# The expert loop's turn from half 0 to half 1: half 0's last groups in turns with half 1's first three, and two separate root chains

## The chip, the core and the metric

The kernel runs on one core of a Trainium2 chip. The metric is the device time of one execution in microseconds (us), the median of several runs. The engines' names in the rows are PE (TensorE), PEld (TensorE's weight loads), DVE (VectorE), ACT (ScalarE), POOL (GpSimd) and SP (SyncE, which only issues DMAs here). ACTq marks DMAs that ScalarE issues.

## The reference

The program is a small "macaron" stack on x of 2 x 1024 tokens with 128 channels: a squared-ReLU feed-forward, softmax attention, the feed-forward again, an expert layer, linear attention, and the same expert layer again.

```python
x = x + 0.5 * ffn0(_layernorm(x))
x = x + attn0(_layernorm(x))
x = x + 0.5 * ffn0(_layernorm(x))
x = x + 0.5 * experts(_layernorm(x))
x = x + linear_attention(_layernorm(x))
x = x + 0.5 * experts(_layernorm(x))
```

The change touches only `experts`:

```python
logits = x_flat @ Wr + br                       # 16 experts
topk_w, topk_idx = top_k(softmax(logits), 2)    # weights made to sum to 1
h = gelu(_layernorm(x_flat @ W1[e] + b1[e], g1[e], be1[e]))
y = sum over the 2 chosen e of topk_w * (h @ W2[e] + b2[e])
```

## The kernel before, in words

The tokens are worked on in two halves of 1024 (the batch's two sequences). Both expert stages run the same code. For each half VectorE works out a slot for each token and choice, so that the tokens of one expert lie together, padded to tiles of 128 rows. GpSimd then sends the rows there with 16 indirect DMAs (`moe_pool_send`, L1157), SyncE loads them back as tiles (L1185), the loop below works on them, ScalarE's queue stores the results (L1192), and GpSimd fetches each token's two rows with 16 indirect DMAs (`moe_pool_fetch`, L1173). It fetches for half 0 once all of half 0's stores have landed, then for half 1 once all of half 1's have. VectorE adds them to x (L1456, L1461).

There are 31 tiles for each half, in 8 groups of 4 (`NGR`; the last has 3). The loop runs over 16 groups: 0 to 7 are half 0's, 8 to 15 half 1's. A group u passes these steps, by the names of the code:

- TensorE: `turn_in(u)` (L1211), 4 transposes of the loaded rows; waits for the load.
- ScalarE: `rows(u)` (L1347), copies them from PSUM.
- TensorE: `hidden(u)` (L1228), the product with the tile's own W1; waits for `rows(u)` and, as it writes the PSUM bank that group u - 4 used, for that group to be scaled.
- VectorE: `summed(u)` (L1406), statistics of each tile; then one root chain of 16 small instructions (L1419 to L1422, then `rsqrt` L233 to L239) for a pair of groups; then `scaled(u)` (L1430).
- TensorE: `turn(u)` (L1238), 4 transposes; ScalarE: `gelu(u)` (L1357), one ACTIVATE for each tile.
- TensorE: `out(u)` (L1252), the product with W2; waits for `gelu(u)` and, since there is one bank for it, for `out_in(u - 1)`.
- ScalarE: `out_in(u)` (L1366), copy to SBUF; then `store(u)` (L1192).

Each engine does its instructions in the order written, so a wait in one holds up all behind it. `LEAD` is 3: TensorE does `hidden(u + 3)` ahead of `turn(u)`. Only group 8 is treated apart before: its `turn_in` and `rows` stand behind `out(3)` and `out_in(3)`, since half 1's rows come late. VectorE takes the groups as 0, then (1, 2), (3, 4), (5, 6), (7, 8), ... (13, 14), then 15, with one root chain for each.

Of the kernel before, what the change touches and what calls it, by code (L numbers as in the profile page):

```python
# [57 lines left out]
def build(nc, A):  # L58
    with ExitStack() as ctx:
# [3 lines left out]
        def sem(name):  # L63
            return ctx.enter_context(nc.semaphore(name))
# [292 lines left out]
        class Ffn:  # L357
# [3 lines left out]
            k, r, v = sem("f_k"), sem("f_r"), sem("f_v")  # L361
# [602 lines left out]
        NGR = (NTL + 3) // 4  # L964
        LEAD = 3
# [234 lines left out]
        def moe_tensor(pe, pair, between):  # L1200
            u0 = NGR * pair[0].i
            last = u0 + 2 * NGR
            where = {}

            def turn_in(u):
                m, g = pair[(u - u0) // NGR], (u - u0) % NGR
                pe.wait_ge(t.xg[g], 16 * (m.i + 1))
                if u >= u0 + 2:
                    pe.wait_ge(t.xtc, u - 1)
                for j in range(tiles_in(g)):  # L1210
                    ins = pe.transpose(ps[:, TURN_IN_BANKS[u % 2], j * P:(j + 1) * P], t_xg[:, m.b, g, j, :], cc("ident"))  # L1211
                ins.then_inc(t.xt, 1)

            def hidden(u):
                m, g = pair[(u - u0) // NGR], (u - u0) % NGR
                k = tiles_in(g)
                if g == 0:
                    pe.wait_ge(m.tab, m.i + 1)
                regs = [pe.alloc_register(f"e{u}_{j}") for j in range(4)]
                pe.load(regs, r_tab[m.b][0:1, 4 * g:4 * g + 4])  # L1220
                at = [pe.snap(r, min_val=0, max_val=(NE - 1) * P) for r in regs]
                where[u] = regs, at
                pe.wait_ge(t.xtc, u + 1)
                if u >= u0 + 4:
                    pe.wait_ge(t.z, u - 3)
                bank = HIDDEN_BANKS[u % 4]
                for j in range(k):
                    ins = pe.matmul(ps[:, bank, j * P:(j + 1) * P], t_xt[:, u % 2, j * P:(j + 1) * P],  # L1228
                                    w1[:, :, :].rearrange("c e f -> c (e f)")[:, bass.ds(at[j], P)], start=True, stop=True)
                ins.then_inc(t.h, 1)  # L1230

            def turn(u):
                g = (u - u0) % NGR
                if u > u0 and u != last - 2:
                    pe.wait_ge(t.ac, u if u < last - 1 else u - 1)
                pe.wait_ge(t.z, u + 1)
                for j in range(tiles_in(g)):
                    ins = pe.transpose(ps[:, turn_bank(last - u), j * P:(j + 1) * P], t_z[:, u % 4, j, :], cc("ident"))  # L1238
                ins.then_inc(t.zt, 1)

            def out(u):
                m, g = pair[(u - u0) // NGR], (u - u0) % NGR
                k = tiles_in(g)
                pe.wait_ge(t.ac, u + 1)
                bank = out_bank(last - u)
                if u == last - 1:
                    pe.wait_ge(t.yc, u - 1)
                elif u >= u0 + 1 and u != last - 2:
                    pe.wait_ge(t.yc, u)
                regs, at = where.pop(u)  # L1250
                for j in range(k):
                    ins = pe.matmul(ps[:, bank, j * P:(j + 1) * P], t_a[:, u % 2, j * P:(j + 1) * P],  # L1252
                                    w2[:, :, :].rearrange("c e f -> c (e f)")[:, bass.ds(at[j], P)], start=True, stop=True)
                ins.then_inc(t.y, 1)
                for r in regs:
                    pe.free_register(r)

            def counts_read(m):
                pe.wait_ge(m.pick, m.i + 1)
                pe.wait_ge(m.gsel, m.i + 1)  # L1260

            pe.wait_ge(pair[0].slot, pair[0].i + 1)
            counts_read(pair[0])
            pe.wait_ge(s_w1, 1)
            turn_in(u0)
            keep_clock(pe, HIDDEN_BANKS[3], 2)
            hidden(u0)
            turn_in(u0 + 1)
            between(0)
            turn_in(u0 + 2)  # L1270
            hidden(u0 + 1)
            turn_in(u0 + 3)
            hidden(u0 + 2)
            between(1)
            keep_clock(pe, HIDDEN_BANKS[3], 6)
            pe.wait_ge(pair[1].slot, pair[1].i + 1)
            for u in range(u0, last - LEAD):
                hidden(u + LEAD)
                if u + LEAD + 1 < last and u + LEAD + 1 != u0 + NGR:
                    turn_in(u + LEAD + 1)  # L1280
                turn(u)
                if u == u0:
                    counts_read(pair[1])
                else:
                    out(u - 1)
                if u + LEAD + 1 == u0 + NGR:
                    turn_in(u + LEAD + 1)
            out(last - LEAD - 1)
            turn(last - 3)
            turn(last - 2)  # L1290
            out(last - 3)
            turn(last - 1)
            out(last - 2)
            out(last - 1)
# [43 lines left out]
        def moe_scalar(act, pair, between):  # L1338
            u0 = NGR * pair[0].i
            last = u0 + 2 * NGR  # L1340

            def rows(u):
                k = tiles_in(u)
                act.wait_ge(t.xt, u + 1)
                if u >= u0 + 2:
                    act.wait_ge(t.h, u - 1)
                nc.scalar.activation(t_xt[:, u % 2, 0:P * k], ps[:, TURN_IN_BANKS[u % 2], 0:P * k], ACT.Identity,  # L1347
                                     bias=cc("ident")[:, 0:1]).then_inc(t.xtc, 1)

            def gelu(u):  # L1350
                m, g = pair[(u - u0) // NGR], (u - u0) % NGR
                act.wait_ge(t.zt, u + 1)
                if u >= u0 + 2:
                    act.wait_ge(t.y, u - 1)
                for j in range(tiles_in(g)):
                    k = 4 * g + j
                    ins = nc.scalar.activation(t_a[:, u % 2, j * P:(j + 1) * P], ps[:, turn_bank(last - u), j * P:(j + 1) * P], ACT.Gelu,  # L1357
                                               bias=r_sel[m.b][:, 1, k:k + 1], scale=r_sel[m.b][:, 0, k:k + 1])
                ins.then_inc(t.ac, 1)

            def out_in(u):
                k = tiles_in(u)
                act.wait_ge(t.y, u + 1)
                if u >= 4:
                    act.wait_ge(t.ys[u % 4], 16 * (u // 4))
                nc.scalar.activation(t_y[:, u % 4, 0:k, :], ps[:, out_bank(last - u), 0:P * k].rearrange("p (j f) -> p j f", f=P), ACT.Copy)\  # L1366
                    .then_inc(t.yc, 1)

            for u in range(u0, u0 + LEAD + 1):
                rows(u)  # L1370
            between()

            def store(u):
                moe_scalar_store(act, pair[(u - u0) // NGR], (u - u0) % NGR)

            for u in range(u0, last - LEAD):
                if u >= u0 + 2:
                    store(u - 2)
                if u + LEAD + 1 < last and u + LEAD + 1 != u0 + NGR:
                    rows(u + LEAD + 1)  # L1380
                gelu(u)
                if u > u0:
                    out_in(u - 1)
                if u + LEAD + 1 == u0 + NGR:
                    rows(u + LEAD + 1)
            out_in(last - 4)
            store(last - 5)
            gelu(last - 3)
            store(last - 4)
            gelu(last - 2)  # L1390
            out_in(last - 3)
            gelu(last - 1)
            store(last - 3)
            out_in(last - 2)
            store(last - 2)
            out_in(last - 1)
            store(last - 1)

        def moe_vector_tiles(dve, vs, pair, slots, behind):
            u0 = NGR * pair[0].i  # L1400
# [31 lines left out]
                    bc(t_rs[:, at, pos:pos + k].unsqueeze(2), [P, k, P]), ALU.mult).then_inc(t.z, 1)  # L1432

            last = u0 + 2 * NGR - 1
            for u in range(u0 - 1, last + 1, 2):
                groups = range(max(u, u0), min(u + 1, last) + 1)
                for v in groups:
                    summed(v)
                dve.wait_ge(t.ss, groups[-1] + 1)
                if u < u0:  # L1440
                    vs.finish_both(slots, Chain(rstds(groups[0], groups[-1])))
                else:
                    vs.finish(Chain(rstds(groups[0], groups[-1])))
                for v in groups:
                    scaled(v)
# [1076 lines left out]
```

## Time and profile before

| what | value |
|---|---|
| median of 3 runs | 601.48 us (598.48 to 602.64) |
| the profiled execution's own time | 601.2 us |
| its span in the trace | 599.0 us |
| busy: PE, DVE, ACT, POOL | 81%, 78%, 52%, 27% of the span |
| first expert loop in the trace | about 322 to 386 us |
| second expert loop | about 509 to 570 us |
| fetches for half 1 to the end | 573.4 to 599.0 us |

The busy shares are means over the whole program, in which attention takes the larger part (to about 290 us). For the change the two expert loops and what follows each of them have to be read by themselves, instruction by instruction.

### The profile page before, as it was taken

Reading aid. Unit: us, or ns where it says so; the run is one execution under the profiler, and the core shown is the slowest. Engines: PE = TensorE matmul, PEld = TensorE weight load, DVE = VectorE, ACT = ScalarE, POOL = GpSimd, SP = SyncE. Lnnn points to the kernel's source line nnn. Section 1 sums busy time; section 2 is a strip of 40 time slices with the busy share of each in tenths; the row PEclk is TensorE's granted clock in tenths of the full one; section 3 lists DMA queues with packets and bytes.
Section 4 is the critical chain, followed back from the end, with each engine's and each line's share of the span. In section 5 each row is a group of like instructions: output and inputs, shape, how many; then the busy total and the mean of one; then the engine's idle time right before and its main releaser. Section 6 shows DMA issues by size and latency. Waiting matters only on the chain.

```text
span 599.0 us, 9248 instructions
## 1 busy us (share of the span) xinstructions
PE 487.4 (81%) x2996; PEld 259.4 (43%) x2996; DVE 468.1 (78%) x1248; ACT 312.5 (52%) x613; POOL 158.8 (27%) x198
## 2 busy tenths in 40 slices
PE   6787989999999999899788789748786887789720
PEld 3452422222222232244364679535435444679610
DVE  4978898988878988465887978697977776888852
ACT  2355456777776777688232658527143202468800
POOL 5020030010000110001274702773101055630775
PEclk8888999999999999999987979987989888999975
DMA  6006500049705003000235295511000012454542
GB/s 209 3 1 162 96 2 0 19 103 194 259 2 146 2 0 72 2 0 2 67 131 163 82 277 162 154 48 27 2 1 0 2 36 68 145 166 139 155 127 66
DMA packets 55356, 49.31 MB, mean 82 GB/s; under 512 B 4958, under 2 KB 47502, under 8 KB 54926
## 3 DMA queue, kind: packets, MB, share of 16 engines
q1 hardware_dynamic: 34686, 31.15, 18.8%
q0 software_dynamic: 4240, 9.45, 5.7%
q10 hardware_dynamic: 16384, 8.13, 4.5%
q8 instruction: 25, 0.41, 0.3%
q14 instruction: 21, 0.17, 0.1%
HBM read 25.85 MB, written 20.59 MB: 78 GB/s over the span
## 4 chain that ended last, share of the span: by engine, by line
PE 37%; DVE 28%; POOL 11%; issue 9%; ACT 9%; DMA 4%; ACTq 1%; SPq 0%; POOLq 0%; DVEq 0%
PE ps L814 9%; DVE arena L862 8%; PE ps L804 7%; PE ps L761 7%; POOL rows_in L1157 7%; ACT arena L1357 5%; POOL arena L1173 2%; DVE stat L257 2%; ACT arena L1366 1%; POOL small L249 1%; DMA row<-in_rows 1%; PE ps L575 1%; DVE arena L1905 1%; DMA arena<-rows_in 1%; DVE xl L285 1%
## 5 line engine op out<-in xcount | busy, mean ns | idle before, releaser
L862 DVE TENSOR_REDUCE arena<-ps 128x1 f32<-128x1024 f32 x128 | 150.8, 1219 | 25.0 <-PE ps L761 24.7
L927 ACT ACTIVATE arena<-ps 128x512 f32<-128x512 f32 x256 | 138.4, 602 | 55.1 <-PE ps L804 52.8
L804 PE MATMUL ps<-arena 99*128 99x512 bf16 x256 | 85.5, 383 | 1.1 <-ACT arena L927 1.0
L761 PE MATMUL ps<-arena 96*128 96x512 bf16 x256 | 76.5, 381 | 7.0 <-DVE arena L862 6.7
L1173 POOL DMA_INDIRECT arena<-rows_out,route x64 | 61.2, 956 | 66.4 <-DMA rows_out<-arena 47.1
L1157 POOL DMA_INDIRECT rows_in<-xl,route x64 | 62.4, 976 | 55.2 <-DVE route L1113 37.1
L814 PE MATMUL ps<-arena 128*32 128x512 f32 x512 | 68.2, 605 | 1.9 <-ACT arena L923 1.3
L804 PEld LDWEIGHTS ps<-arena 99*128 99x128 bf16 x256 | 22.2, 98 | 72.9 <-ACT arena L927 48.9
L249 POOL TENSOR_TENSOR small<-small,nhalf 128x8 f32<-128x8 f32 x11 | 18.2, 1657 | 123.4 <-DVE small L271 123.3
L1357 ACT ACTIVATE arena<-ps,route 128x128 f32<-128x128 f32 x124 | 46.4, 461 | 5.7 <-PE ps L1238 5.7
L202 PE MATMUL ps<-zerob 128*128 128x512 bf16 x148 | 43.7, 448 | 1.4 <-POOL zerob L2100 1.4
L942 POOL CAST arena<-arena 128x16 bf16<-128x16 f32 x7 | 2.2, 320 | 150.0 <-issue 95.7
L1252 PE MATMUL ps<-w,arena 128*128 x248 | 35.8, 289 | 6.4 <-ACT arena L1357 3.4
L1228 PE MATMUL ps<-w,arena 128*128 x248 | 36.2, 290 | 4.6 <-ACT arena L1347 3.8
L1347 ACT ACTIVATE arena<-ps,cst 128x512 f32<-128x512 f32 (+1 forms) x32 | 21.5, 674 | 34.7 <-PE ps L1211 30.2
L761 PEld LDWEIGHTS ps<-arena 96*128 96x128 bf16 x256 | 21.9, 98 | 40.5 <-DVE arena L862 18.7
L1252 PEld LDWEIGHTS ps<-w,arena 128*128 128x128 f32 x248 | 31.7, 200 | 9.5 <-issue 8.7
L1228 PEld LDWEIGHTS ps<-w,arena 128*128 128x128 f32 x248 | 31.4, 197 | 9.7 <-issue 9.3
L1406 DVE BATCH_NORM_STATS2 arena<-ps 128x6 f32<-128x128 f32 x124 | 26.5, 282 | 9.2 <-PE ps L1228 9.2
L294 ACT ACTIVATE xl<-x,small 128x128 f32<-128x128 f32 x40 | 16.4, 485 | 22.8 <-DVE small L280 22.8
L202 PEld LDWEIGHTS ps<-zerob 128*128 128x128 bf16 x148 | 16.0, 113 | 21.9 <-issue 10.6
L1238 PE MATMUL ps<-cst,arena 128*128 128x128 f32 x124 | 19.6, 284 | 5.9 <-DVE arena L1430 5.6
(276 smaller groups left out, 786.6 us busy)
## 6 DMA issues: line engine op xcount, KB each, us to landing
arena<-rows_in SPq DMA_DIRECT2D x28, 256.0 KB, 4.5
rows_out<-arena ACTq DMA_DIRECT2D x28, 256.0 KB, 2.6
rows_in<-zerob SPq DMA_DIRECT2D x2, 1920.0 KB, 11.1
arena<-att_parts SPq DMA_DIRECT2D x12, 256.0 KB, 8.9
arena<-in_consts SPq DMA_DIRECT2D x2, 1024.0 KB
arena<-zerob SPq DMA_DIRECT2D x1, 2048.0 KB, 10.5
arena<-att_parts SPq DMA_DIRECT2D x14, 128.0 KB, 8.1
att_parts<-arena SPq DMA_DIRECT2D x6, 256.0 KB
```

What stands on the lines that cost most here:

```text
L202: pe.matmul(ps[:, bank, :], zerob[:, 0:P], zerob[:, :], start=True, stop=True)
L761: ins = pe.matmul(ps[:, bank + keys, :], a_qs[0:96, b, h, j * P:(j + 1) * P], a_ks[0:96, b, h, keys * 512:(keys + 1) * 512], start=True, s ...
L804: pe.matmul(ps[:, score_bank(n), :], a_ks[0:99, b, h0 + h4, i * P:(i + 1) * P], a_qs[0:99, b, h0 + h4, half * 512:(half + 1) * 512], start ...
L814: ins = pe.matmul(ps[32 * h4:32 * h4 + 32, VALUE_BANK, :], a_v[:, TB * b + i, h0 + h4, :], a_p[:, (4 * step + h4) % 16, :], start=(i == 0) ...
L862: nc.vector.tensor_reduce(a_nm[:, o % 2, k:k + 1], ps[:, bank:bank + 2, :].rearrange("p a b -> p (a b)"), AX.X, ALU.max, negate=True).then ...
L927: nc.scalar.activation(a_p[:, n % 16, :], ps[:, score_bank(n), :], ACT.Exp, scale=0.25).then_inc(a.ex, 1)
L1157: pool.indirect_dma_start(out=rows_in[b], out_offset=bass.IndirectOffsetOnAxis(ap=r_slot[b][:, k * TB + j:k * TB + j + 1], axis=0), in_=xl ...
L1173: pool.indirect_dma_start(out=t_yg[:, b, k, j, :], out_offset=None, in_=rows_out[b], in_offset=bass.IndirectOffsetOnAxis(ap=r_slot[b][:, k ...
L1228: ins = pe.matmul(ps[:, bank, j * P:(j + 1) * P], t_xt[:, u % 2, j * P:(j + 1) * P], w1[:, :, :].rearrange("c e f -> c (e f)")[:, bass.ds( ...
L1252: ins = pe.matmul(ps[:, bank, j * P:(j + 1) * P], t_a[:, u % 2, j * P:(j + 1) * P], w2[:, :, :].rearrange("c e f -> c (e f)")[:, bass.ds(a ...
L1357: ins = nc.scalar.activation(t_a[:, u % 2, j * P:(j + 1) * P], ps[:, turn_bank(last - u), j * P:(j + 1) * P], ACT.Gelu, bias=r_sel[m.b][:, ...
L1406: ins = nc.vector.bn_stats(t_ss[:, at, pos + j, :], ps[:, HIDDEN_BANKS[u % 4], j * P:(j + 1) * P])
```

## The change

TensorE and ScalarE: where half 0 ends, the order of the steps is written anew. For k = 0, 1, 2 TensorE now does `out(4 + k)`, `turn(5 + k)`, `turn_in(8 + k)`, `hidden(8 + k)`, and ScalarE `out_in(4 + k)`, `store(3 + k)`, `rows(8 + k)`, `gelu(5 + k)`. Then follow `out(7)`, `turn_in(11)` and ScalarE's `store(6)`, `out_in(7)`, `store(7)`, `rows(11)`, and from group 8 on the loop as it was. VectorE: the pair (7, 8) is taken apart into 7 alone and 8 alone, each with its own statistics, root chain and scaling.

```diff
@@ -1274,17 +1274,30 @@   (moe_tensor)
             pe.wait_ge(pair[1].slot, pair[1].i + 1)
-            for u in range(u0, last - LEAD):
+            n = u0 + NGR
+            for u in range(u0, n - LEAD):
                 hidden(u + LEAD)
-                if u + LEAD + 1 < last and u + LEAD + 1 != u0 + NGR:
+                if u + LEAD + 1 < n:
                     turn_in(u + LEAD + 1)
                 turn(u)
                 if u == u0:
                     counts_read(pair[1])
                 else:
                     out(u - 1)
-                if u + LEAD + 1 == u0 + NGR:
+            for k in range(LEAD):
+                out(n - 4 + k)
+                turn(n - 3 + k)
+                turn_in(n + k)
+                hidden(n + k)
+            out(n - 1)
+            turn_in(n + LEAD)
+            for u in range(n, last - LEAD):
+                hidden(u + LEAD)
+                if u + LEAD + 1 < last:
                     turn_in(u + LEAD + 1)
+                turn(u)
+                if u > n:
+                    out(u - 1)
             out(last - LEAD - 1)
@@ -1373,16 +1386,32 @@   (moe_scalar)
-            for u in range(u0, last - LEAD):
+            n = u0 + NGR
+            for u in range(u0, n - LEAD):
                 if u >= u0 + 2:
                     store(u - 2)
-                if u + LEAD + 1 < last and u + LEAD + 1 != u0 + NGR:
+                if u + LEAD + 1 < n:
                     rows(u + LEAD + 1)
                 gelu(u)
                 if u > u0:
                     out_in(u - 1)
-                if u + LEAD + 1 == u0 + NGR:
+            for k in range(LEAD):
+                out_in(n - 4 + k)
+                store(n - 5 + k)
+                rows(n + k)
+                gelu(n - 3 + k)
+            store(n - 2)
+            out_in(n - 1)
+            store(n - 1)
+            rows(n + LEAD)
+            for u in range(n, last - LEAD):
+                if u >= n + 2:
+                    store(u - 2)
+                if u + LEAD + 1 < last:
                     rows(u + LEAD + 1)
+                gelu(u)
+                if u > n:
+                    out_in(u - 1)
             out_in(last - 4)
@@ -1432,12 +1461,13 @@   (moe_vector_tiles)
             last = u0 + 2 * NGR - 1
-            for u in range(u0 - 1, last + 1, 2):
-                groups = range(max(u, u0), min(u + 1, last) + 1)
+            n = u0 + NGR
+            for groups in ([u0], [u0 + 1, u0 + 2], [u0 + 3, u0 + 4], [u0 + 5, u0 + 6], [u0 + 7],
+                           [n], [n + 1, n + 2], [n + 3, n + 4], [n + 5, n + 6], [n + 7]):
                 for v in groups:
                     summed(v)
                 dve.wait_ge(t.ss, groups[-1] + 1)
-                if u < u0:
+                if groups[0] == u0:
```

ScalarE before, first expert stage, from `gelu(4)` to `gelu(6)` (L1357 is `gelu`, L1366 `out_in`, L1347 `rows`, the DMA `store`):

```order
102 L1357 ACTIVATE arena<-ps,route 128x128 x4
103 L1366 ACTIVATE arena<-ps 128x512
104 L1347 ACTIVATE arena<-ps,cst 128x512
105 L1192 DMA rows_out<-arena 128x4x128
106 L1347 ACTIVATE arena<-ps,cst 128x512
107 L1357 ACTIVATE arena<-ps,route 128x128 x4
108 L1366 ACTIVATE arena<-ps 128x512
109 L1192 DMA rows_out<-arena 128x4x128
110 L1347 ACTIVATE arena<-ps,cst 128x512
111 L1357 ACTIVATE arena<-ps,route 128x128 x4
```

And the same place in the changed kernel, where the lines have moved (L1370 is `gelu`, L1379 `out_in`, L1360 `rows`):

```order
102 L1370 ACTIVATE arena<-ps,route 128x128 x4
103 L1379 ACTIVATE arena<-ps 128x512 x2
104 L1192 DMA rows_out<-arena 128x4x128
105 L1360 ACTIVATE arena<-ps,cst 128x512
106 L1370 ACTIVATE arena<-ps,route 128x128 x4
107 L1379 ACTIVATE arena<-ps 128x512
108 L1192 DMA rows_out<-arena 128x4x128
109 L1360 ACTIVATE arena<-ps,cst 128x512
110 L1370 ACTIVATE arena<-ps,route 128x128 x4
```

Before, the copy that follows a `gelu(u)` is `out_in(u - 1)`, and `rows` of group u + 4 or later goes ahead of `gelu(u)`. Now, between `gelu(4)` and `gelu(5)`, there stand `out_in(3)`, `out_in(4)` and `rows(8)`; and between `gelu(5)` and `gelu(6)` there stand `out_in(5)`, of the very group that has just been through `gelu`, and `rows(9)`.

TensorE before, the same stage, from the end of `out(3)` to `turn(5)` (L1211 is `turn_in`, L1220 to L1228 `hidden`, L1238 `turn`, L1252 `out`):

```order
639 L1252 MATMUL ps<-w,arena 128x128
640 L1211 MATMUL ps<-cst,arena 128x128 x4
641 L1220 TENSOR_LOAD route
642 L1221 ISA
643 L1228 ISA
644 L1228 MATMUL ps<-w,arena 128x128
...
650 L1228 MATMUL ps<-w,arena 128x128
651 L1211 MATMUL ps<-cst,arena 128x128 x4
652 L1238 MATMUL ps<-cst,arena 128x128 x4
```

And now, from the end of `out(4)` to the start of `out(5)`:

```order
647 L1252 MATMUL ps<-w,arena 128x128
648 L1238 MATMUL ps<-cst,arena 128x128 x4
649 L1211 MATMUL ps<-cst,arena 128x128 x4
650 L1220 TENSOR_LOAD route
651 L1221 ISA
652 L1228 ISA
653 L1228 MATMUL ps<-w,arena 128x128
...
659 L1228 MATMUL ps<-w,arena 128x128
660 L1252 REGISTER_ALU
```

`out(4)` and `turn(5)` have moved ahead of `turn_in(8)`, and no second `turn_in` stands between `hidden(8)` and the next `out`. The same order stands in the second stage.

## Rows read from the trace of the kernel before

**Rows 1.** Chain of waits, second expert stage (start us, us, what).
```profile
533.07 2.81 DMA arena<-rows_in
...
569.88 2.22 DMA rows_out<-arena
```

**Rows 2.** Timeline of VectorE, second stage (start, length, engine, line, what, [idle before <-releaser]).
```profile
535.02 1.29 DVE L1430 TENSOR_TENSOR arena<-ps,arena 128x512 f32<-128x512 f32 x2
...
538.62 0.89 DVE L1406 BATCH_NORM_STATS2 arena<-ps 128x6 f32<-128x128 f32 x4 [1.71 <-PE ps L1228]
...
543.74 1.67 DVE L1406 BATCH_NORM_STATS2 arena<-ps 128x6 f32<-128x128 f32 x8
...
549.76 1.67 DVE L1406 BATCH_NORM_STATS2 arena<-ps 128x6 f32<-128x128 f32 x8
...
561.83 0.69 DVE L1406 BATCH_NORM_STATS2 arena<-ps 128x6 f32<-128x128 f32 x3
...
565.59 0.56 DVE L1430 TENSOR_TENSOR arena<-ps,arena 128x384 f32<-128x384 f32 x1
```

**Rows 3.** Timeline of ScalarE, second stage.
```profile
535.51 0.61 ACT L1366 ACTIVATE arena<-ps 128x512 f32<-128x512 f32 x1
...
550.41 0.37 ACTq L1192 DMA_DIRECT2D rows_out<-arena  x1
...
551.46 1.50 ACT L1357 ACTIVATE arena<-ps,route 128x128 f32<-128x128 f32 x4
...
553.94 0.69 ACT L1347 ACTIVATE arena<-ps,cst 128x512 f32<-128x512 f32 x1 [0.50 <-ACT arena L1366]
554.53 1.50 ACT L1357 ACTIVATE arena<-ps,route 128x128 f32<-128x128 f32 x4
...
561.35 0.61 ACT L1366 ACTIVATE arena<-ps 128x512 f32<-128x512 f32 x1
```

**Rows 4.** Timeline of TensorE, second stage.
```profile
535.92 0.66 PE L1211 MATMUL ps<-cst,arena 128*128 128x128 f32 x4 [0.93 <-DMA arena<-rows_in]
537.43 1.15 PE L1228 MATMUL ps<-w,arena 128*128 x8 [0.85 <-ACT arena L1347]
538.42 0.60 PE L1211 MATMUL ps<-cst,arena 128*128 128x128 f32 x4
538.86 0.60 PE L1238 MATMUL ps<-cst,arena 128*128 128x128 f32 x4
...
562.20 1.13 PE L1252 MATMUL ps<-w,arena 128*128 x8 [1.36 <-ACT arena L1366]
563.16 1.04 PE L1238 MATMUL ps<-cst,arena 128*128 128x128 f32 x8
```

**Rows 5.** Timeline of GpSimd at the end: half 0's last fetch, half 1's first two.
```profile
572.15 0.96 POOL L1173 DMA_INDIRECT arena<-rows_out,route  x1 [0.30 <-DMA rows_out<-arena]
573.42 0.96 POOL L1173 DMA_INDIRECT arena<-rows_out,route  x1 [0.30 <-issue]
575.44 0.94 POOL L1173 DMA_INDIRECT arena<-rows_out,route  x1 [1.06 <-issue]
```

**Rows 6.** Timelines of ScalarE, TensorE and VectorE, first expert stage.
```profile
347.97 0.61 ACT L1366 ACTIVATE arena<-ps 128x512 f32<-128x512 f32 x1
...
349.34 1.12 PE L1211 MATMUL ps<-cst,arena 128*128 128x128 f32 x4 [1.94 <-DMA arena<-rows_in]
351.31 2.07 PE L1228 MATMUL ps<-w,arena 128*128 x8 [0.85 <-ACT arena L1347]
...
360.35 0.89 DVE L1406 BATCH_NORM_STATS2 arena<-ps 128x6 f32<-128x128 f32 x4 [0.93 <-PE ps L1228]
```

**Rows 7.** Windows of 3 us: length, PE, PEld, DVE, ACT, POOL busy (count), PEclk, DMA share, GB/s.
```profile
351.00:354.00 3.00, 2.69 (x12) 2.70 (x13) 0.58 (x3) 0.18 (x1) 0.00 (x0) 0.50 1.09 318
...
522.00:525.00 3.00, 1.21 (x6) 1.24 (x7) 2.83 (x12) 1.07 (x4) 2.33 (x3) 0.72 0.13 44
...
564.00:567.00 3.00, 1.71 (x14) 1.40 (x13) 2.66 (x14) 3.00 (x9) 2.13 (x3) 1.00 0.79 223
```

## The prediction, made before the changed kernel ran

> **What bounds the kernel now.** I read the chain of waits first, from its end backwards. It ends with half 1's 16 fetches, which GpSimd issues one after the other; ahead of these stands the landing of half 1's last store, at 569.88 + 2.22 = 572.10, and further up the load of half 1's first rows, landed at 533.07 + 2.81 = 535.88 [rows 1]. Next, GpSimd's timeline: half 0's last fetch starts at 572.15, half 1's first at 573.42, 1.27 later, as fetches follow each other [rows 5]. So there two things end almost together: half 0's fetches, and half 1's stores 1.3 us before half 1's first fetch starts. Making half 0's part earlier can win at most those 1.2 us; anything that makes half 1's last store later than about 573.3 is paid in full.
>
> What sets that store is the loop between 535.88 and 569.88. In its steady part VectorE works without idle time: from one pair's statistics to the next it takes 549.76 - 543.74 = 6.02 us, 3.01 for a group [rows 2]. ScalarE takes 554.53 - 551.46 = 3.07 for a group [rows 3]. Both are full, so a delay of the pair (9, 10) reaches group 15 whole. At the turn between the halves there is slack: VectorE ends group 6 and sums group 7 by 537, then waits 1.71 us for `hidden(8)` [rows 2], and TensorE waits 0.93 us for the rows [rows 4].
>
> **VectorE's part of the change.** The pair (7, 8) becomes two chains: one more set of 16 small instructions in each stage. A group alone costs 565.59 + 0.56 - 561.83 = 4.3 us (group 15, three tiles) [rows 2], against 6.0 for a pair. In the second stage group 7 starts at 535.02 + 1.29 = 536.3 with its statistics and is scaled at about 540.6; group 8 then takes 0.85 for statistics, 3.1 for the chain and 0.6 for the scaling, and VectorE is free for group 9 at about 545.0, where it was at 543.74 [rows 2]. By itself that costs half 1 1.25 us.
>
> **The order on TensorE and ScalarE.** The new inner order makes a ring with nothing in parallel: `gelu(u)`, `out(u)`, `turn(u + 1)`, `turn_in(u + 4)`, `rows(u + 3 or 4)`, and only then the next `gelu`. (For k = 1 it is `gelu(5)`, `out(5)`, `turn(6)`, `turn_in(9)`, `rows(9)`, `gelu(6)`.) Its length, from rows: 0.12 from ScalarE's end to TensorE's start (536.62 + 0.69 to 537.43; the 0.69 is a `rows` copy's length [rows 3], the other end [rows 4]), 0.96 from `out` to the next transposes (562.20 to 563.16), 0.44 for the first transposes (538.42 to 538.86), 0.60 for the second and 0.04 to ScalarE [rows 4], 0.59 from `rows` to `gelu` (553.94 to 554.53) and 1.50 for `gelu` [rows 3]: 4.25 us instead of 3.07. `out_in` and `store` fit beside the transposes.
>
> Start of the ring in the second stage: `out(4)` needs its one bank, that is `out_in(3)`, which ends at 535.51 + 0.61 = 536.12 [rows 3]; such a handover took 0.24 (561.35 + 0.61 to 562.20 [rows 3, 4]). So `out(4)` at 536.36, `turn(5)` at 537.32, `turn_in(8)` at 537.76 (where it started at 535.92), `rows(8)` at 538.40, `gelu(5)` at 538.99. Two rings on, `gelu(7)` starts at 547.49; its `rows(10)` started 0.59 earlier and ends at 547.59, `hidden(10)` runs from 547.71 for 1.15 to 548.86, and its statistics end 0.89 later, at about 549.8. Before they ended at 543.74 + 1.67 = 545.4 [rows 2]. **The pair (9, 10) is 4.4 us later**, which swallows VectorE's own 1.25. From there on the two kernels have the same order. `hidden(12)` has one more such step and comes at about 555.0, when VectorE is ready for it at 554.95: nothing to add or to regain.
>
> Half 1's last store then lands at 572.10 + 4.4 = 576.5, and half 1's first fetch starts at about 576.6 instead of 573.42: **+3.2 us at the end** (4.4 less the 1.3 of slack, and 0.1 for the handover). Half 0's fetches gain nothing: `gelu(7)`, of three tiles, ends at 548.6, then 0.12 + 0.9 for `out(7)` and 0.5 for its copy, and the store goes at 550.2, where it went at 550.41 [rows 3].
>
> **The first stage** has the same ring, but another starting point: the rows came later against the rest (TensorE idle 1.94 us), and TensorE then ran at a granted clock of 0.50, the 1.2 GHz level, so that `hidden(8)` took 2.07 instead of 1.15 us [rows 4, 6, 7]. The kernel before already pays for that: VectorE waited 0.93 for `hidden(10)` and ended its statistics at 360.35 + 0.89 = 361.24 [rows 6]. Now `out_in(3)` ends at 347.97 + 0.61 = 348.58, `out(4)` starts at 348.82, `turn_in(8)` at 350.22, `gelu(5)` at 351.45, `gelu(7)` 8.5 later at 359.95, `hidden(10)` ends at 361.32, its statistics at 362.25: **+1.0 us**, if TensorE stays at 2.4 GHz. I take this, as `out(4)` now fills part of the idle time that stood before the fall. After this stage TensorE's b2 product and VectorE's additions stand behind group 15, so the 1.0 is passed on. Half 0's fetches start some 3 us earlier here; nobody waits for them.
>
> **Sum:** +1.0 + 3.2 = +4.2 us. The profiled execution took 601.2, so 605.4; it lies 0.3 under the median of the runs, 601.48, and on that scale the forecast is **605.7 us**, 0.7% slower. A difference under 1%, 6 us, is about what a measurement of this kernel can't tell from none.
>
> **The clock** is the unknown. A ring keeps TensorE busy for about 3 of 4.25 us, with idle pieces of about 1 us. Near the end of the loop it was busy 1.71 of 3 us and stayed at 1.00; around 523 it was busy 1.21 of 3 and fell (0.72) [rows 7]. The ring is nearer to the first, so I take the high level. At the low one a ring would cost 0.85 more for `out`, 0.4 and 0.5 for the transposes (1.12 against 0.66) [rows 4, 6], some 1.7 us, and the low level held for about 7 us in the first stage, so about 2.3 us for each stage where it falls; nothing excludes it in both. The Trainium skill, "TensorE: Matmul & The Clock Gate", in "HAM oscillation — how this bites in real kernels" and in "Part 4: PE-mode transpose", has idle gaps between bursts bring the clock down, and says that transposes don't count as busy; by that, the new order, which pulls the matmuls apart with waits and transposes, would lose the level. The 1.00 of the window from 564, which has transposes and gaps of 1.3 us too, speaks against it as a certainty.
>
> **Rivals.**
> - *Clock falls, slower by over 1%.* The ring's gaps bring TensorE to 1.2 GHz in one stage (605.7 + 2.3 = 608.0) or in both (610.3). It decides from about 607.5. For it: the fall at 523 and in the first stage. Against: the window from 564. Chance 0.27.
> - *No ring: VectorE alone sets the pace.* If ScalarE and TensorE overlap more than I think, so that `hidden(10)` is there when VectorE has done group 9, half 1 is 1.25 later in the second stage (landing 573.35, first fetch 573.5, so +0.1), and in the first stage the wait of 0.93 goes (-1.0): 600.6 to 601. It would show as no DVE idle ahead of group 10. Against it: the written order. Chance 0.12; a gain of over 1% would need more than the 1.2 us that the end has to give, and there is no place for it: 0.02.
> - *The ring is there, but what follows absorbs it.* The first stage's 1.0 is lost in waits of linear attention, and the unexplained 1.06 us between half 1's first two fetches [rows 5] goes when these start later: 601.5 + 3.2 - 1.1 = 603.6. Chance 0.12.
> - The forecast itself has 0.47.
>
> **Range and chances.** The rivals reach from 600.6 to 610.3; runs of this kernel scatter by 1.5 to 3 us around their median. 600.5 to 609.5 leaves out the lower half of the second rival and the double fall. Slower by over 1% (from 607.5): most of the first rival and a little of the forecast, 0.26. Faster by over 1%: 0.03. Within 1%: 0.71.
>
> **What would show it.** Right: in both stages ScalarE's `gelu` of groups 5, 6, 7 start 4.2 to 4.3 us apart; VectorE idles ahead of group 10's statistics, which end near 549.8 - 550.8 (second stage, with the first stage's shift); 6.0 us for a pair after that; GpSimd waits for the landing of half 1's last store, with idle time between the halves' fetches of over 3 us. Wrong: `gelu` 3.1 us apart; or the granted clock at 0.50 for several us after 350 or 540; or half 1's first fetch directly behind half 0's last.

## The result, and the profile after

The changed kernel took 605.73 us (median of 8 runs, 604.99 to 606.88), the kernel before 601.24 us (median of 8, 598.13 to 603.0; three of the eight are the runs of the table above): a ratio of 1.0071, 95% interval 1.0047 to 1.0094. The forecast was 605.7. The profiled execution took 606.88 us, its span is 605.1 us.

ScalarE after, second expert stage (start, duration, instruction; in brackets the idle time before it and what ended it), against [rows 3]:

```profile
535.66 1.50 ACT L1370 ACTIVATE arena<-ps,route 128x128 f32<-128x128 f32 x4 [0.59 <-PE ps L1238]
...
539.05 0.60 ACT L1379 ACTIVATE arena<-ps 128x512 f32<-128x512 f32 x1 [1.40 <-PE ps L1252]
...
539.93 0.69 ACT L1360 ACTIVATE arena<-ps,cst 128x512 f32<-128x512 f32 x1 [0.28 <-PE ps L1211]
540.51 1.50 ACT L1370 ACTIVATE arena<-ps,route 128x128 f32<-128x128 f32 x4
...
544.77 1.50 ACT L1370 ACTIVATE arena<-ps,route 128x128 f32<-128x128 f32 x4
...
548.91 1.15 ACT L1370 ACTIVATE arena<-ps,route 128x128 f32<-128x128 f32 x3
...
551.66 0.37 ACTq L1192 DMA_DIRECT2D rows_out<-arena  x1
```

L1370 is now `gelu`, L1379 `out_in`, L1360 `rows`. `gelu(4)` is the first row; `gelu(5)`, `gelu(6)` and `gelu(7)` start at 540.51, 544.77 and 548.91, 4.26 and 4.14 us apart, where one took 3.07 before. The last row is `store(7)`.

TensorE after, the same stretch, against [rows 4]:

```profile
535.30 1.13 PE L1252 MATMUL ps<-w,arena 128*128 x8
...
537.89 1.13 PE L1252 MATMUL ps<-w,arena 128*128 x8 [1.46 <-ACT arena L1379]
538.85 0.60 PE L1238 MATMUL ps<-cst,arena 128*128 128x128 f32 x4
539.29 0.60 PE L1211 MATMUL ps<-cst,arena 128*128 128x128 f32 x4
540.74 1.15 PE L1228 MATMUL ps<-w,arena 128*128 x8 [0.85 <-ACT arena L1360]
542.14 1.13 PE L1252 MATMUL ps<-w,arena 128*128 x8 [0.24 <-ACT arena L1370]
...
549.14 1.15 PE L1228 MATMUL ps<-w,arena 128*128 x8 [0.85 <-ACT arena L1360]
```

This is the ring: `out(4)` waits 1.46 us for the copy of `out(3)` (the first row), then `turn(5)`, `turn_in(8)`, a wait of 0.85 for `rows(8)`, `hidden(8)`, and `out(5)` only when `gelu(5)` is done. `hidden(10)`, the last row, comes two turns of the ring later.

VectorE after, against [rows 2] (L1435 statistics, L1459 scaling):

```profile
542.57 0.56 DVE L1459 TENSOR_TENSOR arena<-ps,arena 128x384 f32<-128x384 f32 x1
543.04 0.88 DVE L1435 BATCH_NORM_STATS2 arena<-ps 128x6 f32<-128x128 f32 x4
...
547.61 0.88 DVE L1435 BATCH_NORM_STATS2 arena<-ps 128x6 f32<-128x128 f32 x4
550.34 0.89 DVE L1435 BATCH_NORM_STATS2 arena<-ps 128x6 f32<-128x128 f32 x4 [1.84 <-PE ps L1228]
...
555.57 1.89 DVE L1435 BATCH_NORM_STATS2 arena<-ps 128x6 f32<-128x128 f32 x8
```

Group 7 is scaled alone, group 8 alone, group 9 is summed; then VectorE waits 1.84 us for `hidden(10)`. So its own second chain is hidden behind the ring, not added to it.

GpSimd after, second stage, against [rows 5], and the same place in the first stage:

```profile
573.32 0.95 POOL L1173 DMA_INDIRECT arena<-rows_out,route  x1 [0.30 <-issue]
578.92 0.95 POOL L1173 DMA_INDIRECT arena<-rows_out,route  x1 [4.65 <-DMA rows_out<-arena]
581.35 0.95 POOL L1173 DMA_INDIRECT arena<-rows_out,route  x1 [1.48 <-issue]
```
```profile
391.10 0.95 POOL L1173 DMA_INDIRECT arena<-rows_out,route  x1 [3.62 <-DMA rows_out<-arena]
```

Half 0's fetches are done at 574.27 and GpSimd waits 4.65 us for half 1's last store. The chain of waits (start, duration, step) names the same:

```profile
571.05 1.79 ACT arena L1370 x5
576.05 1.96 DMA rows_out<-arena
578.92 0.95 POOL arena L1173
579.88 1.48 issue
```

The store lands at 578.01 (576.05 + 1.96), and the fetch starts 0.91 later. First stage, TensorE, ScalarE and VectorE, against [rows 6], and two windows, against [rows 7]:

```profile
347.43 1.13 PE L1252 MATMUL ps<-w,arena 128*128 x8
349.92 1.13 PE L1252 MATMUL ps<-w,arena 128*128 x8 [1.36 <-ACT arena L1379]
...
352.78 1.15 PE L1228 MATMUL ps<-w,arena 128*128 x8 [0.85 <-ACT arena L1360]
```
```profile
352.55 1.50 ACT L1370 ACTIVATE arena<-ps,route 128x128 f32<-128x128 f32 x4
356.80 1.50 ACT L1370 ACTIVATE arena<-ps,route 128x128 f32<-128x128 f32 x4
```
```profile
362.37 0.89 DVE L1435 BATCH_NORM_STATS2 arena<-ps 128x6 f32<-128x128 f32 x4 [1.76 <-PE ps L1228]
```
```profile
351.00:354.00 3.00, 2.08 (x17) 1.65 (x15) 2.59 (x17) 2.64 (x6) 0.00 (x0) 1.00 1.13 334
...
546.00:549.00 3.00, 2.05 (x17) 1.68 (x15) 2.29 (x10) 1.54 (x4) 0.00 (x0) 1.00 0.20 58
```

The same ring, 4.25 us, and the granted clock is 1.00 in it (2.4 GHz): `hidden(8)` took 1.15 us, where it took 2.07 before.

**A yardstick.** Both kernels do `out(3)` and, after group 15, TensorE's b2 product; between them lies all that changed. From start to start, and on to half 1's first fetch in the second stage (us):

| kernel | first stage, `out(3)` to b2 | second, `out(3)` to b2 | second, `out(3)` to first fetch |
|---|---|---|---|
| before | 346.27 to 385.83: 39.56 | 533.86 to 570.06: 36.20 | 39.56 |
| changed | 347.43 to 388.26: 40.83 | 535.30 to 576.23: 40.93 | 43.62 |
| changed, again | 348.81 to 389.69: 40.88 | 535.85 to 576.70: 40.85 | 43.55 |
| one ring | 347.67 to 386.10: 38.43 | 535.44 to 573.85: 38.41 | 41.53 |
| two rings | 349.00 to 387.91: 38.91 | 537.75 to 576.71: 38.96 | 42.21 |

"One ring" and "two rings" are kernels of the experiments below, with one or two turns of the ring instead of three.

The 6.1 us between the two spans are: 1.16 before the first `out(3)`, which the change does not touch; 1.27 in the first stage; -0.99 from there to the second stage's `out(3)`; 4.06 to the first fetch; 0.41 between it and the second (1.48 against 1.06 of idle time); 0.19 after that. The medians differ by 4.5.

### The profile page after: what moved, and what is told of

Read it like the earlier page. It is cut to its first block, busy times and chain, and to the rows that moved or that the text cites. A ratio compares the mean times of both kernels' runs of the same rounds, so it can differ in the third digit from the quotient of the medians.

```text
span 605.1 us, 9282 instructions
## 1 busy us (share of the span) xinstructions
PE 485.2 (80%) x2996; PEld 256.9 (42%) x2996; DVE 473.7 (78%) x1280; ACT 313.9 (52%) x613; POOL 159.0 (26%) x198
## 4 chain that ended last, share of the span: by engine, by line
PE 41%; DVE 34%; ACT 10%; issue 7%; POOL 5%; DMA 3%; ACTq 1%; SPq 0%; POOLq 0%; DVEq 0%
PE ps L814 9%; DVE arena L862 8%; PE ps L804 7%; PE ps L761 7%; ACT arena L1370 5%; DVE stat L257 2%; POOL arena L1173 2%; PE ps L1252 2%; POOL small L249 2%; PE ps L1228 2%; ACT arena L1379 1%; DVE arena L1435 1%; PE ps L1671 1%; PE ps L575 1%; DVE arena L1935 1%
## 5 line engine op out<-in xcount | busy, mean ns | idle before, releaser
L1370 ACT ACTIVATE arena<-ps,route 128x128 f32<-128x128 f32 x124 | 46.5, 462 | 5.1 <-PE ps L1238 4.6
L1228 PE MATMUL ps<-w,arena 128*128 x248 | 35.3, 285 | 11.7 <-ACT arena L1360 10.9
L202 PE MATMUL ps<-zerob 128*128 128x512 bf16 x148 | 41.9, 434 | 1.4 <-POOL zerob L2130 1.4
L1252 PE MATMUL ps<-w,arena 128*128 x248 | 34.5, 281 | 10.1 <-ACT arena L1379 5.5
L1228 PEld LDWEIGHTS ps<-w,arena 128*128 128x128 f32 x248 | 30.3, 191 | 17.3 <-issue 17.0
L1360 ACT ACTIVATE arena<-ps,cst 128x512 f32<-128x512 f32 (+1 forms) x32 | 21.5, 675 | 29.5 <-PE ps L1211 26.5
L1252 PEld LDWEIGHTS ps<-w,arena 128*128 128x128 f32 x248 | 30.1, 191 | 13.5 <-issue 13.1
L1435 DVE BATCH_NORM_STATS2 arena<-ps 128x6 f32<-128x128 f32 x124 | 26.7, 282 | 7.5 <-PE ps L1228 7.3
L294 ACT ACTIVATE xl<-x,small 128x128 f32<-128x128 f32 x40 | 16.4, 485 | 22.7 <-DVE small L280 22.7
L1379 ACT ACTIVATE arena<-ps 128x512 f32<-128x512 f32 (+1 forms) x32 | 19.0, 593 | 14.1 <-PE ps L1252 14.1
```

The source lines that it names most:

```text
L202: pe.matmul(ps[:, bank, :], zerob[:, 0:P], zerob[:, :], start=True, stop=True)
L1435: ins = nc.vector.bn_stats(t_ss[:, at, pos + j, :], ps[:, HIDDEN_BANKS[u % 4], j * P:(j + 1) * P])
```

## The experiments

The theory: the order of TensorE and ScalarE makes a serial ring, and it alone costs; VectorE's separate chains are hidden. The rivals: the chains cost as well; one stage only pays; the clock has a part. Each kernel was timed in turns with the kernel before. Three chips served: on one the kernel before took 601.51 us, near the 601.24 of the result above, on the two others 684.14 and 682.33. So only ratios of one chip are compared. The expectations are given in the numbers of the 601 us chip, and four of these kernels (the order alone, the chains alone and one stage at a time) ran on the slow chips only.

**The order alone** (684 us chip, then again on the 682 us chip): VectorE's pairs as before, the rest as changed.

```diff
-            for groups in ([u0], [u0 + 1, u0 + 2], ... [u0 + 7], [n], [n + 1, n + 2], ... [n + 7]):
+            for u in range(u0 - 1, last + 1, 2):
+                groups = range(max(u, u0), min(u + 1, last) + 1)
```

> The new order on TensorE and ScalarE alone; VectorE keeps the pair (7, 8). Theory A (the ring gelu, out, turn, turn_in, rows of 4.25 us sets when hidden(10) is there): all of the loss stays, since group 10 comes no earlier; first stage +1.0, second stage's first fetch for half 1 about 3 us later against the loop's start; 605 to 606 us, ratio 1.006 to 1.008; gelu of groups 5, 6, 7 start 4.2 to 4.3 apart. Theory B (VectorE's extra root chain of 3.1 us, twice, is what costs): at least half of the loss goes, 603 us or less.

> The new order alone again, for the condition in which before takes about 601 us. Theory A (ring): as the whole change, ratio 1.006 to 1.009; from the last send to TensorE's b2 product 43.4 to 45.2 us in the second stage, as in the changed kernel, against 39.8 of before. Theory B (the extra chain): half of that or less.

Measured: 692.46 against 684.14, 1.0116 (1.0084 to 1.0149); again 689.56 against 682.33, 1.0117 (1.0076 to 1.0158); 5 and 6 executions. More than the whole change cost on the 601 us chip; the direction is as expected, the size was missed. ScalarE, second stage, `gelu(5)` to `gelu(7)`:

```profile
609.82 1.50 ACT L1370 ACTIVATE arena<-ps,route 128x128 f32<-128x128 f32 x4
614.08 1.50 ACT L1370 ACTIVATE arena<-ps,route 128x128 f32<-128x128 f32 x4
618.22 1.15 ACT L1370 ACTIVATE arena<-ps,route 128x128 f32<-128x128 f32 x3
```

The ring has the same length there, 4.26 and 4.14, with VectorE's old pairs: it comes from the order.

**VectorE's chains alone** (the same two chips): the reverse of that diff on the kernel before.

```diff
-            for u in range(u0 - 1, last + 1, 2):
-                groups = range(max(u, u0), min(u + 1, last) + 1)
+            for groups in ([u0], [u0 + 1, u0 + 2], ... [u0 + 7], [n], [n + 1, n + 2], ... [n + 7]):
```

> VectorE's groups 7 and 8 with chains of their own alone; TensorE and ScalarE in the order of before. Theory A: in the second stage half 1's last store 0.7 to 1.25 us later, which the 1.3 us between its landing and the first fetch for half 1 takes up; in the first stage VectorE had waited for hidden(10) anyway: 601.2 to 601.9 us, ratio 1.000 to 1.001. Theory B: 603 to 606 us.

> The separate chains alone again, for the condition near 601 us. Theory A: ratio 0.999 to 1.002; from the last send to the b2 product 40.5 to 41.0 us in the second stage (0.7 to 1.25 over before's 39.8), taken up by the slack ahead of half 1's first fetch. Theory B: 1.004 or more.

Measured: 684.21 against 684.14, 1.0008 (0.9985 to 1.0031); again 683.07 against 682.33, 1.0022 (0.9997 to 1.0047). At most 0.5%, and nothing by both intervals. The rival that the chains cost falls for these chips. Both repeats were meant for a chip near 601 us, which did not come up, so the spans that their expectations name could not be compared.

Why is the order dearer on these chips? Two rows of the 682 us chip. GpSimd with the order alone, second stage, and TensorE's `hidden(8)` with the kernel before's order (chains alone), first stage:

```profile
661.56 0.95 POOL L1173 DMA_INDIRECT arena<-rows_out,route  x1 [22.20 <-DMA rows_out<-arena]
```
```profile
369.62 1.15 PE L1228 MATMUL ps<-w,arena 128*128 x8 [1.40 <-ACT arena L1347]
```

GpSimd waits 22 us for half 1's last store, and with the chains alone, in the old order, it waits 20.09 us there, so no slack stands before the end. And the old order's `hidden(8)` took 1.15 here, not the 2.07 of [rows 6]: the clock does not fall at this place, so the new order has no fall to take away. Both allowances that lowered the cost on the 601 us chip are missing, and 4.4 for each stage would be 8.8; measured were 8.3 and 7.2 us. The next experiment has rows for it.

**One stage at a time** (684 us chip): the whole change under a condition on the stage, the old code otherwise.

```diff
+            if (pair[0].i == 0) == True:      # second kernel: == False
                 n = u0 + NGR
...
+            else:
+                for u in range(u0, last - LEAD):
...
```

> The whole change in the first expert stage only. Theory A: the forecast's first term, +1.0 us if TensorE's clock stays high in that loop (602.2), +3.3 if it falls. gelu of 5, 6, 7 are 4.25 apart in the first stage and 3.07 apart in the second; GpSimd goes from half 0's fetches to half 1's without a wait in the second stage. If the loss were all from the end of the program (theory C: only the last landing counts), 601.2.

> The whole change in the second expert stage only. Theory A: the forecast's second term, +3.2 us (604.4), or +3.6 with a gap between the first two fetches for half 1 that is 0.4 longer, as the changed kernel showed; half 1's last store lands 4.4 us later against the load of its first rows, and 1.3 of it is slack. The two stage-only kernels' losses add up to the whole, 4.5 within 1.5 us.

Measured: first stage alone 687.45, 1.0056 (1.0036 to 1.0076), +3.3 us; second alone 688.93, 1.0064 (1.0038 to 1.009), +4.8 us. The sum, 8.1, is the order's 8.3: the stages add up and nothing between absorbs them. The first stage cost 3.3 where I expected 1.0, for the reason just given. The yardstick from `out(3)` to the b2 product, on this chip, agrees. Each of the two kernels has one stage with the old code: 55.41 us (first) and 54.53 (second). With the new code these stages took 58.75 and 58.75, and 59.27 and 58.84 with the order alone: 3.3 to 3.9 us more in the first and 4.2 to 4.3 in the second. So the 8.3 us are two stages' worth, with one profile for each kernel, and with long waits of another kind inside these spans (the last section).

**The changed kernel again, one ring and two rings** (601 us chip): the three turns cut to one or two, then the order of before; VectorE's chains stay separate.

```diff
-            for k in range(LEAD):
+            for k in range(1):                # two rings: range(2)
                 out(n - 4 + k)
...
-            out(n - 1)
-            turn_in(n + LEAD)
-            for u in range(n, last - LEAD):
+            turn_in(n + 1)
+            for u in range(n - LEAD + 1, last - LEAD):
```

> The changed kernel itself, once more beside before, on the chip of this call. If the times are near 601 again: ratio 1.005 to 1.009. If they are near 684, as in the first four experiments, where GpSimd waited some 18 to 22 us for half 1's last store and so no 1.3 us of slack stand between them: theory A says that each stage's loop then costs 4.4 us with nothing taken off (8 to 9 us, ratio 1.012 to 1.013), as the order alone did (1.0116).

> The change with two of its three rings: k = 0 and 1 in turns, then the order of before. Theory A: group 9 comes by the ring, group 10 does not wait for a third; half 1's last store 2.2 us later than before in the second stage (less the slack of 1.3 where it exists), half of the whole change's 4.4: ratio 1.001 to 1.004 near 601 us, 1.005 to 1.008 near 684 us. Theory B (the extra root chain costs): as the whole change.

> The change with one ring: k = 0 in turns, then the order of before; VectorE's two chains stay. Theory A: half 1's last store 1.0 us later than before in the second stage, all within the slack where it exists; in the first stage out(4) and turn(5) fill TensorE's wait for the rows, and if its clock then does not fall, 1.6 us are won: 599.6 to 601.9 near 601 us; ratio 1.000 to 1.004 near 684 us. Theory B: as the whole change.

Measured: the changed kernel 606.27 against 601.51, 1.0085 (1.0058 to 1.0113); two rings 606.79, 1.009 (1.0064 to 1.0117); one ring 603.85, 1.0045 (1.0012 to 1.0078). Two rings as slow as three was not expected. The yardstick above has the answer in part. In each of the two stages three rings took 40.8 to 40.9 us, two 38.9, one 38.4: the third turn costs 2, the second only 0.5. `out(4)` and the b2 product of one ring, second stage:

```profile
538.00 1.13 PE L1252 MATMUL ps<-w,arena 128*128 x8 [1.45 <-ACT arena L1377]
...
573.85 3.70 PE L1317 MATMUL ps<-b2d,route 128*128 128x512 f32 x8 [0.52 <-DVE route L1330]
```

So in the stages fewer rings are cheaper, 1.9 to 2.5 us for each stage. But against the kernel before the second stage still took 2.2 us more with one ring and 2.8 with two, where I expected its last store 1.0 and 2.2 later. VectorE, one ring, second stage (L1452 scaling, L1428 statistics):

```profile
547.13 0.69 DVE L1452 TENSOR_TENSOR arena<-ps,arena 128x512 f32<-128x512 f32 x1
547.74 1.67 DVE L1428 BATCH_NORM_STATS2 arena<-ps 128x6 f32<-128x128 f32 x8
```

It goes from the scaling of group 8 to the statistics of (9, 10) without waiting for `hidden(10)`, and it had no idle time since 537.72, where it scaled (5, 6). So with one turn it is no longer the ring that sets when (9, 10) is done, but VectorE with its two separate chains. Three turns of the ring hide them, one does not. (Part of the 2.2 is where VectorE stood: it began to scale (5, 6) 2.28 behind `out(3)` here and 1.16 in the kernel before. One turn with the pair (7, 8) kept was not run.)

The rest of what the fewer rings win is lost between the stages: from the first stage's b2 product to the second stage's `out(3)` the changed kernel took 147.0 and 146.2 us, one ring 149.3, two rings 149.8. The code of that stretch, linear attention and the second routing, is the same in all of them. It can be cut in two at the VectorE instruction (L280) that waits 1.49 us for GpSimd, at 460.88 in the kernel before. Beside each part stands TensorE's granted clock in a piece of it, 55 to 60 and 100 to 110 us behind the b2 product:

| kernel | b2 to L280 (us) | clock, 55 to 60 | L280 to `out(3)` (us) | clock, 100 to 110 |
|---|---|---|---|---|
| before | 75.05 | 0.66 | 72.98 | 1.00 |
| before with the fill (below) | 75.08 | 0.66 | 73.01 | 1.00 |
| changed | 72.99 | 1.00 | 74.05 | 0.71 |
| changed, again | 72.77 | 1.00 | 73.39 | 0.90 |
| one ring | 75.36 | 0.66 | 73.98 | 0.66 |
| two rings | 75.87 | 0.69 | 73.97 | 0.66 |

The length of each part goes with the clock in it: where the first piece held some time at the 1.2 GHz level, its part took 2.1 to 3.1 us more, and where the second held more of it, about 1. These are the pieces in which the kernels differ most, not the only ones. One and two rings met both falls, the changed kernel only the second, the kernel before only the first. Why the clock fell in one kernel and not in another is open, and with one or two profiles for each it is not shown that the kernel decides it.

**Work to hold the clock** (601 us chip), on the kernel before: eight matmuls on zeros in the idle time ahead of the first stage's `turn_in(8)`.

```diff
                 if u + LEAD + 1 == u0 + NGR:
+                    if pair[0].i == 0:
+                        keep_clock(pe, HIDDEN_BANKS[0], 8)
                     turn_in(u + LEAD + 1)
```

> The kernel before, with 8 matmuls on zeros put ahead of turn_in(8) in the first stage, where TensorE waited 1.94 us for half 1's rows. If TensorE's fall to 1.2 GHz there cost the kernel before 2 to 2.5 us, as the forecast's first stage assumes: 598.7 to 599.2 (ratio 0.996), no window at a granted clock of 0.50 between 348 and 357, hidden(8) 1.15 us long. If the fall hides behind VectorE: 601.2.

Measured: 601.02 against 601.51, 0.9984 (0.9954 to 1.0014), no change. TensorE, first stage:

```profile
348.91 1.13 PE L1252 MATMUL ps<-w,arena 128*128 x8
350.09 1.67 PE L202 MATMUL ps<-zerob 128*128 128x512 bf16 x7
351.60 0.60 PE L1211 MATMUL ps<-cst,arena 128*128 128x128 f32 x4
353.06 1.15 PE L1228 MATMUL ps<-w,arena 128*128 x8 [0.86 <-ACT arena L1349]
```

The clock held: `hidden(8)` took 1.15. From `turn_in(8)` to the b2 product it took 386.00 - 351.60 = 34.40 us, in the kernel before 385.83 - 349.34 = 36.49, and in its second stage, at the high level, 570.06 - 535.92 = 34.14. The fall costs 2.1 to 2.3 us. But `turn_in(8)` came at 351.60 instead of 349.34, and what the clock gave was lost again: the fill itself took 1.5 us (350.09 to 351.60), and `out(3)`, ahead of it, had started 2.64 later than in the kernel before (348.91 against 346.27). So how much holding the clock would give by itself is not settled.

**The ring made shorter** (682 us chip): in each turn TensorE does `turn_in(n + k)` ahead of `turn`, so that `rows` can start 0.44 earlier.

```diff
                 out(n - 4 + k)
-                turn(n - 3 + k)
                 turn_in(n + k)
+                turn(n - 3 + k)
                 hidden(n + k)
```

> The changed kernel with turn_in(8 + k) ahead of turn(5 + k) on TensorE, which takes one link of 0.44 us out of each of the three rings. Theory A: gelu of groups 5, 6, 7 start 3.8 instead of 4.25 apart; half 1's last store 0.85 to 1.3 us earlier in each stage than in the changed kernel: 603.8 to 604.6 near 601 us, ratio 1.004 to 1.006. Theory B (VectorE): no difference from the changed kernel.

Measured: 686.7 against 682.33, 1.0066 (1.0041 to 1.009), where the order alone had 1.0117 on this chip: some 2.9 us less (the two intervals overlap a little). The changed kernel itself did not run there, so this compares with the order alone. Its `gelu(5)` to `gelu(7)`, second stage:

```profile
604.08 1.51 ACT L1370 ACTIVATE arena<-ps,route 128x128 f32<-128x128 f32 x4
607.95 1.51 ACT L1370 ACTIVATE arena<-ps,route 128x128 f32<-128x128 f32 x4
611.81 1.16 ACT L1370 ACTIVATE arena<-ps,route 128x128 f32<-128x128 f32 x3
```

3.87 and 3.86 us instead of 4.26 and 4.14: the ring's length is a sum of its links. One link less of 0.44 made a turn 0.4 shorter. From `out(3)` to the b2 product it took 58.27 and 57.34 us, the order alone 58.70 and 58.39: 1.5 us less in the two stages together, about half of the 2.9.

**Another way** (682 us chip), without the ring: the order of before on TensorE and ScalarE; VectorE takes 7 alone and then (8, 9), (10, 11) and so on; half 1's stores go from ScalarE's queue to SyncE's.

```diff
-            for u in range(u0 - 1, last + 1, 2):
-                groups = range(max(u, u0), min(u + 1, last) + 1)
+            for groups in ([u0], ... [u0 + 7], [n, n + 1], [n + 2, n + 3], [n + 4, n + 5], [n + 6, n + 7]):
...
+            for g in range(NGR):
+                moe_scalar_store(sp, m3[1], g, True)
```

> A try at a better version: TensorE's and ScalarE's order of before; VectorE takes 7 alone and then (8, 9), (10, 11), (12, 13), (14, 15), as many chains as before; half 1's stores are issued by SyncE's queue, which spares ScalarE 0.44 us for a group. If ScalarE alone set the pace of 3.07, the first stage would win up to 0.7 us, and the second nothing, since GpSimd is busy with half 0's fetches until 573: 600.5 to 601.5, ratio 0.999 to 1.000 near 601 us.

Measured: 679.22 against 682.33, 0.9965 (0.9941 to 0.999): the one version that beat the kernel before, by 3.1 us; up to 0.7 was expected for the 601 us chip. The two edits were not tried apart, nor on the 601 us chip, where half 0's fetches leave at most 1.2 us to win at the end. Which of the two won is open.

## Why the prediction was right

- **The ring** was forecast at 4.25 us and measured at 4.26, 4.14 (second stage, the last group has three tiles) and 4.25 (first). The order alone shows it, with a cost of 3.3 to 4.3 us for each stage on a slow chip, and the shortened ring shows that it is a sum of links.
- **The pair (9, 10)** was to end its statistics at 549.8. It ended at 551.23, and `out(3)` started 1.44 later than before: 549.79. `store(7)`, forecast at 550.2, went at 551.66 - 1.44 = 550.22. The landing of the last store, forecast at 576.5, came at 578.01 - 1.44 = 576.57. That last agreement is partly two errors against each other. The forecast said that `hidden(12)` would add nothing, but the statistics of (11, 12) took 1.89 us instead of 1.67, and the last store was issued at 576.05 - 1.44 = 574.61, 4.73 later than before and not 4.4; its way to the landing took 1.96 instead of 2.22.
- **VectorE's chain, costed at nothing:** the wait of 1.84 for `hidden(10)` shows the cover, and the chains alone changed nothing measurable (1.0008, 1.0022). The rival "no ring" is refuted. The cover is the three turns' own: with one turn VectorE's chains set the pace.
- **The end** was mis-sized: from `out(3)` the first fetch is 4.06 later, not 3.2, because the handover from the landing to GpSimd took 0.91 us and not the 0.1 that I put. So of the 1.3 us of slack that the forecast took off only 0.4 were there: 572.10 + 0.91 = 573.01, against 573.42. The gap between the first two fetches grew by 0.41 instead of going away, so the rival "absorbed" is refuted in that part.
- **The first stage** cost 1.27, forecast 1.0. The rest of its ring's price was paid before as well, by the low clock; the two other chips, where the old order has no fall there, show the full price.
- **The clock** was the rival with a chance of 0.27, and it did not fall: the level is 1.00 through both rings, with TensorE busy 2.0 to 2.1 of 3 us and idle for 0.24 to 1.46 us at a time. The Trainium skill, "TensorE: Matmul & The Clock Gate", "HAM oscillation — how this bites in real kernels", has idle gaps between bursts bring it down, but its case is of waits for DMA that are longer than any idle piece of this ring. That by this section the new order would lose the level was read into it; the trace shows that gaps of 0.24 to 1.46 us, with transposes beside them, did not bring it down here. The price that the forecast put on a fall, 2.3 us for a stage, was not worked out from its terms (they give 1.7 for a turn, and no row shows the 0.85 for `out`); the fill's trace gives 2.1 to 2.3.
- **By luck:** from the first stage's b2 product to the second's `out(3)` the profiled pair gained 0.99 us, for which the forecast had no term: 2.1 less where the kernel before met a low clock and the changed one did not, 1.1 more where it was the other way round. It offset the two terms that were too small. With two rings the same stretch lost 1.8 against the kernel before. A forecast to 0.1 us is finer than this kernel's own scatter.

## What to carry to other kernels

Before an order is interleaved more finely, follow one item through all engines and add up the links up to the next item of the same kind: if each waits for the one before, the sum is the new period, whatever each engine's busy time says. Pipelining by one group (doing `hidden(u + 3)` ahead of `turn(u)`) was what kept 3.07 us here, and two turns less of the ring gave back some 2.4 us in each stage, until another engine, here VectorE, set the pace. A slack is worth reading with the handover in it: 1.3 us between a landing and the next start were 0.4. A cost that a slack or a low clock hides in one condition is paid in full in another, as the step from 0.7% to 1.2% shows.

## What the runs showed of the hardware

- The same kernel took 601.5 us on one chip and 682 to 684 us on two others. There the waits lie mostly in the expert loops: with VectorE's chains alone it took 71 to 73 us from half 1's last send to the b2 product, where the kernel before took 40 to 43 on the other chip. TensorE in the first stage, with VectorE's chains alone, and the waits of its weight loads for "issue" in the whole program (total, times, longest):

```profile
398.88 1.64 PE L1228 MATMUL ps<-w,arena 128*128 x6 [7.69 <-issue]
407.48 1.11 PE L1238 MATMUL ps<-cst,arena 128*128 128x128 f32 x4 [6.96 <-issue]
```
```profile
PEld ps L1228 <- issue: 53.4, 20, 16.4
DVE arena L1406 <- remote: 45.9, 8, 11.7
```

  The second line is VectorE's statistics, which waited for what the profile calls "remote"; ScalarE did so too, 8.72 and 7.18 us around the two rows above. No semaphore of an engine ends these waits in the profile. What does is open; no run tried it.
- After GpSimd has waited for half 1's last store, its second fetch for half 1 comes with 1.47 or 1.48 us of idle time at the end of the program, in all twelve profiles in which it had idled before the first one, for 0.65 to 22.7 us, on all three chips; without such a wait it was 1.06 [rows 5], and 0.93 with the fill. After the same wait in the first stage it was 0.30. Unexplained.
- TensorE's low level around the first stage's turn costs 2.1 to 2.3 us over the loop, and eight matmuls on zeros held the level without a gain. In the stretch of linear attention the same work took 2.1 to 3.1 us longer in the profiles with a granted clock of 0.66 to 0.69 in a piece of 5 us than in those with 1.00 there.
